# Norms, squares and gates in another order, and GpSimd's lower weight parts behind the first norm, in a two-layer kernel with attention, experts and a gated recurrence

## The reference, cut to what matters

```python
h = layernorm(x) * (1 + ca) + sa
x = x + ga * attention(h)            # layer 0: 16 heads of 8, causal
h = layernorm(x) * (1 + cb) + sb
x = x + gb * experts0(h)             # 8 routed experts (best 2), gelu, 512 wide, and a shared one
h = layernorm(x) * (1 + ca) + sa
x = x + ga * recurrent(h)            # layer 1
h = layernorm(x) * (1 + cb) + sb
x = x + gb * experts1(h)             # 8 experts (best 2), silu(x W1) * (x W3), 256 wide
```

```python
n = rms_norm(h, norm_w)
gate = gelu(n @ fc_gate_w.T + b)
hs = n @ fc_w.T + b
r = sigmoid(n @ fc_r_w.T + b);  i = sigmoid(n @ fc_i_w.T + b)
a = exp(-8 * softplus(alpha) * r)
s = sqrt(1 - a * a) * hs * i
out_t = a_t * out_(t-1) + s_t        # over the 256 tokens
hs2 = out * gate + h
n2 = rms_norm(hs2, norm2_w)
y = ((n2 @ mlp_fc.T + b) * gelu(n2 @ mlp_gate.T + b)) @ out_w.T + b + hs2
```

## Time and profile before

| | |
|---|---|
| runs | 668.92, 670.51, 670.59 us; median 670.51 |
| the profiled execution | 673.97 us, its span 672.2 us |
| TensorE busy | 605.4 us (90%) |
| VectorE busy | 546.4 us (81%) |
| ScalarE busy | 485.9 us (72%) |
| GpSimd busy | 167.2 us (25%) |
| mean granted clock of TensorE | 0.942 of full |

### The profile page before, as it was taken

The page is one execution under the profiler, slowest core; times in us unless marked ns, Lnnn a source line. Parts: engine busy times, 40 slices in busy tenths (PEclk is TensorE's granted clock), DMA queues, the critical chain, the costliest instruction groups (busy, mean ns, idle before and its releaser), DMA issues.

```text
span 672.2 us, 10961 instructions
## 1 busy us (share of the span) xinstructions
PE 605.4 (90%) x3276; PEld 444.0 (66%) x3276; DVE 546.4 (81%) x1344; ACT 485.9 (72%) x857; POOL 167.2 (25%) x144
## 2 busy tenths in 40 slices
PE   8799888888999899999999999781698899999996
PEld 5365555555545688888888887360385788888884
DVE  3657888888866878988988888756899689999997
ACT  4538999999634889999999997677544456666663
POOL 4313322233311115444455432310233000000000
PEclk9669999999987799999999999986699799999998
DMA  7000000000100042022211220000000042222201
GB/s 242 1 0 1 2 2 0 0 0 0 33 1 0 1 161 95 0 95 94 94 43 52 94 86 1 23 1 0 0 1 0 1 152 87 86 87 87 87 0 63
DMA packets 6634, 29.86 MB, mean 44 GB/s; under 512 B 878, under 2 KB 1006, under 8 KB 4399
## 3 DMA queue, kind: packets, MB, share of 16 engines
q1 hardware_dynamic: 6592, 29.37, 12.3%
HBM read 28.18 MB, written 1.19 MB: 44 GB/s over the span
## 4 chain that ended last, share of the span: by engine, by line
PE 62%; DVE 25%; ACT 6%; issue 5%; DMA 1%; POOL 0%; DVEq 0%; SPq 0%; ACTq 0%; POOLq 0%
PE PS L1182 16%; PE PS L1184 16%; PE PS L1183 16%; DVE STAT L860 9%; PE PS L1328 2%; PE PS L1195 2%; DVE RA L880 2%; PE PS L1283 2%; PE PS L1208 2%; DVE SU L886 1%; ACT AR L554 1%; PE PS L1297 1%; ACT RA L612 1%; DVE AR L1141 1%; DVE RA L1148 1%
## 5 line engine op out<-in xcount | busy, mean ns | idle before, releaser
L1001 DVE TENSOR_TENSOR RA<-AR,RA 128x512 fp32r<-128x512 f32 x144 | 138.2, 983 | 27.1 <-ACT RA L512 25.7
L511 ACT ACTIVATE AR<-PS,BI 128x512 f32<-128x512 f32 x144 | 99.4, 690 | 19.2 <-PE PS L1184 12.5
L1182 PE MATMUL PS<-HH,WH 128*128 128x512 f32 x272 | 110.0, 404 | 0.4 <-ACT RA L512 0.3
L1183 PE MATMUL PS<-HH,WL 128*128 128x512 f32 x272 | 107.8, 396 | 0.0
L1184 PE MATMUL PS<-HL,WH 128*128 128x512 f32 x272 | 107.6, 396 | 0.0
L512 ACT ACTIVATE RA<-PS,BI 128x512 fp32r<-128x512 f32 x144 | 98.5, 684 | 0.0
L860 DVE CUSTOM_DVE_ANT_0 STAT<-PS,MQ 128x128 f32<-128x128 f32 (+1 forms) x256 | 76.2, 353 | 21.2 <-PE PS L1284 21.1
L1182 PE MATMUL PS<-RA,WH 128*128 128x512 f32 x208 | 82.6, 397 | 3.5 <-DVE RA L1148 2.0
L1184 PE MATMUL PS<-RA,WH 128*128 128x512 f32 x208 | 81.5, 392 | 0.0
L1183 PE MATMUL PS<-RA,WL 128*128 128x512 f32 x208 | 81.4, 392 | 0.0
L311 POOL TENSOR_TENSOR AR<-AR 128x512 f32<-128x512 f32 x32 | 50.6, 1583 | 113.1 <-DVE AR L813 113.1
(11 more groups left out here) (211 smaller groups left out, 1179.6 us busy)
## 6 DMA issues: line engine op xcount, KB each, us to landing
AR<-comb SPq DMA_DIRECT2D x16, 1024.0 KB, 4.8
WS<-in_w SPq DMA_DIRECT2D x9, 512.0 KB, 5.6
WS<-in_w SPq DMA_DIRECT2D x8, 384.0 KB, 3.1
M<-in_mats SPq DMA_DIRECT2D x1, 1384.0 KB, 10.7
X<-in_xT SPq DMA_DIRECT2D x4, 256.0 KB, 4.5
out_xT<-X SPq DMA_DIRECT2D x4, 256.0 KB, 2.1
AR<-in_wmod SPq DMA_DIRECT2D x1, 768.0 KB, 7.6
KM<-in_kmats SPq DMA_DIRECT2D x1, 162.5 KB
```

The source lines that it names most:

```text
L511: act.activation(G[:, c, :], PS[:, c, :], ACT.Gelu_apprx_tanh, bias=bias).then_inc(s["act"], 1)
L1001: dve.tensor_tensor(out=GL[:, m0 % 2, c, :], in0=G[:, c, :], in1=f(GH[:, m0 % 2, c, :]), op=ALU.subtract).then_inc(s["lo"], 1)
L1182: pe.matmul(out, wh, xh, start=first, stop=False)
L1183: pe.matmul(out, wl, xh, start=False, stop=False)
```

## The change

- GpSimd: L283 waits until the first norm is written (`hn_done` 8). The first three upper parts of norm 1 come ahead of the split of the second expert's weights. Upper parts of norm 3 come ahead of the first splits of layer 1's experts. The fill of ACC goes from GpSimd to ScalarE, as two copies.
- TensorE: `variance(1, 3)` comes ahead of the first four `hidden0` groups; all four `variance(4, t)` come ahead of `mlp_hidden(0)`.
- ScalarE: `square(3, 2)` comes ahead of `inverse(2, 3)`. The four gelu gates come behind the exponentials and the roots, with a table load more, and the squares of norm 4 come behind the gates.
- VectorE: the product with the gate and the sum with the residual become `gated(t)`, called apart from `recurrence(t)`; the four `one_less_square` come first; norm 4's order follows.
- SyncE: the ninth expert's weights are loaded without the row broadcast into WB.

```diff
                 if ne == 9:
-                    later(8, 0)
+                    sp.wait_ge(s["split"], 16)
+                    sp.dma_start(WS[:, 0:width], w[8, :, :]).then_inc(s["w_in"], 16)
...
             gp.wait_ge(l1_split, 1)
+            gp.wait_ge(hn_done, 8)
             gp.tensor_tensor(out=LL[:, :], in0=lm, in1=f(LH[:, :]), op=ALU.subtract).then_inc(l1_split, 1)
...
-                gp.wait_ge(s["acc_init"], 1)
+                gp.wait_ge(s["acc_init"], 2)
...
             split_weights(0, 0, 0, 1024)
+            for t in range(3):
+                split_hidden(1, HN, t)
             gp.wait_ge(moe[0]["w_in"], 32)
             split_weights(0, 1, 1, 1024)
-            for t in range(NBLK):
-                split_hidden(1, HN, t)
-            gp.wait_ge(wo_done, 4)
-            shared_bias = V[:, VAT["b2"] + E0 - 1:VAT["b2"] + E0]
-            gp.tensor_scalar(ACC, shared_bias.to_broadcast([128, TOK]), 1.0, 0.0, ALU.mult, ALU.add)\
-              .then_inc(moe[0]["acc_init"], 1)
+            split_hidden(1, HN, 3)
             experts(0, E0, 1024)
             gp.wait_ge(moe[0]["y"], 4 * E0)
+            for t in range(NBLK):
+                split_hidden(3, XC, t)
             for e in range(2):
                 gp.wait_ge(moe[1]["w_in"], 16 * (e + 1))
                 split_weights(1, e, e, 768)
-            for t in range(NBLK):
-                split_hidden(3, XC, t)
...
             inverse(1, 2)
+            act.wait_ge(wo_done, 4)
+            shared_bias = V[:, VAT["b2"] + E0 - 1:VAT["b2"] + E0]
+            for part in range(2):
+                act.activation(ACC[:, 1024 * part:1024 * part + 1024], shared_bias.to_broadcast([128, 1024]), ACT.Copy)\
+                   .then_inc(moe[0]["acc_init"], 1)
             square(1, XC, 3)
             inverse(1, 3)
...
             inverse(3, 1)
+            square(3, HN, 2)
             inverse(2, 3)
-            for t in (2, 3):
-                square(3, HN, t)
-                inverse(3, t)
-            for i, (p, t) in enumerate(projected):
...
+            inverse(3, 2)
+            square(3, HN, 3)
+            inverse(3, 3)
+            def gates1(which):
+                for i, (p, t) in enumerate(projected):
+                    if p in which:
...
+            gates1((0, 1))
             act.preload_act_table_set("natural_log_exp_and_others")
...
-            root(0)
-            root(1)
+            for t in range(NBLK):
+                root(t)
+            gates1((2,))
+            act.preload_act_table_set("natural_log_exp_and_others")
             square(4, H2, 0)
-            root(2)
-            inverse(4, 0)
-            square(4, H2, 1)
-            root(3)
-            inverse(4, 1)
-            for t in (2, 3):
+            for t in range(1, NBLK):
                 square(4, H2, t)
-                inverse(4, t)
+                inverse(4, t - 1)
+            inverse(4, 3)
...
-            one_less_square(0)
-            one_less_square(1)
+            for t in range(NBLK):
+                one_less_square(t)
             recurrence(0)
-            one_less_square(2)
             recurrence(1)
-            one_less_square(3)
+            recurrence(2)
+            gated(0)
+            recurrence(3)
+            gated(1)
+            gated(2)
+            gated(3)
             rms(4, H2, "norm2", 0)
-            recurrence(2)
+            rms(4, H2, "norm2", 1)
             rest(4, XC, 0)
-            rms(4, H2, "norm2", 1)
-            recurrence(3)
+            rms(4, H2, "norm2", 2)
             rest(4, XC, 1)
-            rms(4, H2, "norm2", 2)
+            rms(4, H2, "norm2", 3)
             rest(4, XC, 2)
-            rms(4, H2, "norm2", 3)
             rest(4, XC, 3)
...
+            variance(1, 3)
             pe.wait_ge(s["split"], 2)
-            hidden0(0, 0, 0)
-            hidden0(0, 0, 1)
-            variance(1, 3)
-            hidden0(0, 0, 2)
-            hidden0(0, 0, 3)
+            for c in range(4):
+                hidden0(0, 0, c)
             router(0, 3)
...
-            for t in range(3):
+            for t in range(NBLK):
                 variance(4, t)
...
-                    if t == 0 and c == 0:
-                        variance(4, 3)
```

More of the change, by code:

```diff
@@ L544, in _ @@
             inverse(3, 1)
+            square(3, HN, 2)
             inverse(2, 3)
-            for t in (2, 3):
-                square(3, HN, t)
-                inverse(3, t)
-            for i, (p, t) in enumerate(projected):
-                if p == 3:
-                    continue
-                act.wait_ge(p1_psum, i + 1)
-                func = (ACT.Sigmoid, ACT.Sigmoid, ACT.Gelu)[p]
-                act.activation(blk((R_, I_, GATE)[p], t), PS[:, i % 8, :], func, bias=vec("pb", p))\
-                   .then_inc(p1_done, 1)
+            inverse(3, 2)
[4 more added lines that the diff above has]
+                    if p in which:
+                        act.wait_ge(p1_psum, i + 1)
+                        func = (ACT.Sigmoid, ACT.Sigmoid, ACT.Gelu)[p]
+                        act.activation(blk((R_, I_, GATE)[p], t), PS[:, i % 8, :], func, bias=vec("pb", p))\
+                           .then_inc(p1_done, 1)
+            gates1((0, 1))
             act.preload_act_table_set("natural_log_exp_and_others")
@@ L1056, in recurrence, with gated @@
                                            initial=0.0, op0=ALU.mult, op1=ALU.add).then_inc(scan_done, 1)
+            def gated(t):
                 dve.wait_ge(scan_done, 2 * t + 2)
```

## The result

The changed kernel takes 652.86 us in the median (652.21 to 656.36, 4 runs), the kernel before in the same job 670.55 (668.92 to 673.49). The ratio is 0.9742, with a 95% interval from 0.9693 to 0.9791: 17.3 us less, and between 14 and 21. Three later repetitions beside other kernels gave 0.9729, 0.9733 and 0.9713. The forecast was 10.5 us less (660.0), its range ended at 655.8. The sign was right, the size was not.

The account below looks back on a forecast made before the run. The prediction took TensorE to carry 62% of the chain, VectorE 25%, so gains ahead of the long TensorE-bound expert stages pass through whole. Terms 3.3 + 1.1 + 3.1 + 3.0 = 10.5 took 670.5 to 660.0 us; range 655.8 to 665.2.

Parts of the forecast that it names:

- norms, gates and recurrence of layer 1: Layer 1, norm 2 through the start of mlp_hidden(1): new orders gain 3.0 us (bounds 0.5 and 4.6).
- start: Kernel start: holding L283 back frees VectorE's L835 and the first normalises, 3.3 us faster (bounds 2.5 and 3.4).
- norms 2 and 3: Layer 1 norms up to the sigmoids' table load: moved splits and earlier square(3,2) bring that load 1.25 us earlier.
- gates and recurrence: Layer 1 behind the sigmoids' table load: exponentials earlier with gates behind the roots, partly lost again; 1.75 us gained.
- Tail: Last attention units: L880 starts 1.0 us earlier once the split moves, plus 0.1 of clock; 1.1 us (bounds 0.5 and 2.7).
- Norm 1: Norm ahead of the first experts: earlier variance(1,3) and no GpSimd ACC fill gain 3.1 us (bounds 1.5 and 4.5).
- the part called clock: Norm ahead of the first experts: TensorE fed almost without a break, low clock partly recovered, taken as 0.3 us.
- the collision: Layer 1 recurrence: GpSimd's second weight split lands on VectorE's first one_less_square, costing 1.9 us (bounds 0 and 2.65).
- the clock comes back as well: Rival: low-clock stretches shrink too and the collision may miss the squares; 14 us faster, 656.5, chance 0.15.
- only the port stalls pay: Rival: shorter port stalls gain, layer 1's reordering gives its start back; 5.8 us faster, 664.7, chance 0.17.
- The slower one: Rival at the start: late L283 delays GpSimd's joins, first scores and attention; 672.5 or more, chance 0.03.
- No change: Rival: VectorE's stalls are slack, as TensorE has other work behind them; 670.5, chance 0.03.

Follow-up runs that it names:

- p4_layer1: Kernel before with only the layer 1 edits (norms 2 to 4, gates, recurrence, GpSimd's order, no ninth-expert row broadcast): ratio 0.9904, 6.4 us faster.
- p1: Kernel before with only L283's wait on the first norm: ratio 0.9947, 3.6 us faster.
- p2: Kernel before with only the second expert's weight split moved behind the third upper part of norm 1: ratio 0.9985, 1.0 us faster.
- p5a: Kernel before with only square(3,2) put ahead of inverse(2,3): ratio 0.9941.
- p6: Kernel before with only gates, roots, gateds and norm 4 in the new order, GpSimd as before: ratio 0.9885, 7.7 us faster.
- f1: Kernel before with 68 unused matmuls into a free PSUM bank in TensorE's recurrence hole, to hold its clock: ratio 0.9987, no difference.
- p5b: Kernel before with only norm 3's upper parts ahead of the weight splits and no ninth-expert row broadcast: ratio 0.9963.

## Why the prediction was wrong

The step that failed is the term "norms, gates and recurrence of layer 1": predicted 3.0, measured 7.5 by the marks and 6.4 (5 to 8) by p4_layer1. The other terms together missed by 1.6. With the means of the stretches over the executions with and without the edits, the sum stands like this. The mean of A without the wait is 175.3 (nine executions), with it 171.3 (ten).

| term | predicted | measured | from |
|---|---|---|---|
| start | 3.3 | 4.0 (p1: 3.6, 2 to 5) | A |
| tail and norm 1 | 1.1 + 3.1 = 4.2 | 4.2 + 0.9 = 5.1 | B: 44.4 to 40.2; C: 9.9 to 9.0 |
| norms 2 and 3 | 1.25 | 3.8 | E: 25.7 to 21.9 |
| gates and recurrence | 1.75 | 3.7 | F: 43.65 to 39.95 |
| sum | 10.5 | 16.6 | ratio: 17.3, 14 to 21 |

G is 176.5 in the mean for both.

- **Start: right.** L835's wait, the cover of L283 (it ended at 27.10, the join began at 28.50), and the small operations that would wait for it (L940) came as written.
- **Tail: right in mechanism**, and 1.0 for 1.1 by p2 (0.3 to 1.7).
- **Norm 1: right in the order of its steps.** The two copies were hidden, `variance(1,3)` moved up by 2.9, the last L675 took 0.69, the cover over the blocked lower parts held. Short was the part called clock: 0.3 was taken for what C shows as 0.9. The bounds of the term, 1.5 to 4.5, held it. But how the gain of B divides isn't shown. The old code at a clock of 0.98 to 1.00 (41.9 to 42.7) against the new (40.2) leaves 1.7 to 2.5 us for the waits, where the sum had 1.0 + 2.9 in tail and norm 1. The rest of the 4.2 would be clock, for which the sum had 0.4. That the two terms came out near may so be luck in part.
- **Norms 2 and 3: the term that was mis-sized**, 1.25 for 3.8. The order worked by the steps forecast: the first projection starts 16.29 behind norm 2's table load instead of 17.96. Two things were missing. First, the base: the stretch in the one execution of before was 24.43, and 25.9 to 26.1 in the five others with that code. An improvement on the mean is 1.3 larger than one on that trace. Secondly, the nine matmuls of the first projections stood under the low clock before (from 439.71 to variance(3,3) at 443.76, 4.05 us) and don't now (425.17 to 428.00, 2.83): 1.2 that the text named for other places and not for this one. The square's place alone (p5a) brought E to 22.62.
- **Gates and recurrence: mis-sized too**, 1.75 for 3.7. The start (exponentials 3.7 earlier) and the collision (first scan 7.50 behind the exponentials, forecast 7.7; 5.8 without the split) were right. The step that failed is "mlp_hidden(0) now starts only behind variance(4,3), at 476.5 ... end near 482.9". That is 24.2 and 30.6 behind the exponentials; it measured 22.70 and 28.05. The operations were charged 0.8 too much up to the last gated (19.74 for 20.5), the variances and inverses 0.7 too much, and the 12 matmuls at the low clock, 1.05 with all they delay, weren't there: mlp_hidden(0) ran at 0.23 us a matmul. One thing was wrong the other way: `mlp_hidden(1)` did still wait for the first product, 0.86 us. In the changed kernel's four executions F is 39.61 and 39.66 where the last variance ran at the full clock, and 40.04 and 40.11 where it didn't.
- **The range** was too narrow on the fast side. The fast bounds of its own terms add up to 3.4 + 2.7 + 4.5 + 4.6 = 15.2 and the range ended at 14.7 (655.8); the measured 17.7 lies outside of both. The rival "the clock comes back as well" had the right direction, but priced its layer 1 part at 1.5 also for a collision that might miss, and the collision came.
- **The rivals:** "only the port stalls pay" is refuted by p4 to p6, most of the gain is in the new orders. The slower one did not come near: 1.4 us were left between L283 and the join. "No change" is refuted by the result itself.

What stays open: in B, C and E the clock's share is read from how length and clock go together over executions of equal code, and no run set the clock there. What decides whether one execution of a stretch meets the low clock and the next doesn't is open too.

## What to carry to other kernels

Compare stages over several executions before sizing a term from one trace: a stretch with holes in it varied by up to 5 us between executions of the same code, one without holes by 0.04. Read the granted clock of the stretch beside its length. Where an instruction of a few columns lasts microseconds, look for what the other engine of the pair runs beside it, and place that work where VectorE is not the chain; there may be no free place, and then it is better left. Filling TensorE's holes to hold its clock can pay only where somebody waits for TensorE, and in the two fills here the clock fell right behind the fill, where somebody did.

## What the runs showed of the hardware that was not expected

- The low clock cost nothing in a hole that another engine set: with 1.00 instead of 0.50 there (f1) the last variance came at the same time to 0.03 us, 33.8 behind the sigmoids' table load. The whole time changed by 0.9 us, inside the noise (0.9967 to 1.0007).
- The same code took 46.43 us at a granted clock of 0.87 and 42.61 at 1.00 (stretch B of p6 and p5b).
- A one-column VectorE operation (L940) lasted 3.69 us, as long as the GpSimd subtraction beside it. L835 (32 columns) took 3.59 beside one of 3.69, L894 (256 columns) 2.56 beside one of 2.36: the length followed the GpSimd instruction and not the columns.
- GpSimd pays as well: its 1,024-column copy and subtraction took 1.48 and 2.68 us beside VectorE's lower parts, 1.04 and 2.35 at 170.60 to 174.08, where VectorE mostly reads PSUM.
- ScalarE fills 1,024 columns from a single one in 0.99 us (two in 1.98).
